# Bank products of a linear-attention memory: 64-row head pairs against 32-row single heads in four row quarters of TensorE

## The reference

```python
sigma_q = elu_plus_one(q)                                   # (b, 16 heads, s, 32)
a_unnorm = jnp.einsum('bhsd,nhde->nbhse', sigma_q, memories)    # 4 banks n, 32x32 per head
norm = jnp.einsum('bhsd,nhd->nbhs', sigma_q, memory_norms)
a = a_unnorm / jnp.clip(norm, EPS, None)[..., None]
a = a * active[:, None, None, None, None]
weights = jax.nn.softmax(bank_weights, axis=-1)
combined = jnp.einsum('nbhse,hn->bhse', a, weights)
out = combined.transpose(0, 2, 1, 3).reshape(b, s, HID) @ Wo.T
```

## Time and profile before

| | |
|---|---|
| median of 3 runs | 1446.71 us (1446.37 to 1449.19) |
| the profiled execution | 1446.95 us |
| its span, first to last instruction | 1445.1 us |
| PE / DVE / POOL / ACT busy | 1400.0 / 876.9 / 544.2 / 509.6 us |
| bank products (L1163) | 768 matmuls of 64x128 by 64x256 |
| DVE's scalings (L910) | 128 of 128x512, 79.5 us |
| PE's granted clock, mean | 0.993 of 2.4 GHz |

### The profile page before, as it was taken

One profiled execution on the slowest core, in us unless ns is written; L12 is line 12 of the kernel. 1 busy time (PEld: TensorE's weight loads), 2 busy tenths in 40 slices (PEclk: granted clock), 3 DMA queues, 4 the chain that ended last, 5 costly groups with the idle time before them and its releaser, 6 DMA issues.

```text
span 1445.1 us, 18902 instructions
## 1 busy us (share of the span) xinstructions
PE 1400.0 (97%) x6890; PEld 1151.9 (80%) x6890; DVE 876.9 (61%) x1255; ACT 509.6 (35%) x794; POOL 544.2 (38%) x363
## 2 busy tenths in 40 slices
PE   7999999998989999999999999999999999999997
PEld 6678888887768888888888887878888888888885
DVE  5577777877576546454555557484654555563644
ACT  4546666666631222122221233332212212222221
POOL 0656566666043333131322335462313133232311
PEclk9999999999999999999999999999999999999999
DMA  7302222203420202020110312230202111020102
GB/s 253 106 21 97 87 87 87 87 29 146 151 90 29 95 0 94 0 94 29 65 65 29 113 40 95 88 124 1 95 6 89 59 36 65 29 94 0 65 0 94
DMA packets 24040, 102.41 MB, mean 71 GB/s; under 512 B 3012, under 2 KB 3524, under 8 KB 14284
## 3 DMA queue, kind: packets, MB, share of 16 engines
q1 hardware_dynamic: 24012, 102.05, 19.0%
HBM read 68.47 MB, written 33.57 MB: 71 GB/s over the span
## 4 chain that ended last, share of the span: by engine, by line
PE 79%; DVE 12%; issue 4%; ACT 3%; DMA 1%; POOL 1%; SPq 0%; DVEq 0%; POOLq 0%; ACTq 0%
PE bank L1085 25%; PE bank L1087 25%; PE bank L1086 25%; DVE banks_r L910 2%; PE bank L1113 1%; DVE h_abs L1037 1%; PE bank L1163 1%; DVE combT_lo L879 1%; DVE one_each L1025 1%; PE bank L1104 1%; DVE x_ring L873 1%; PE bank L1173 1%; DVE pair_lo L1019 1%; DVE ln_raw L757 1%; DVE inv_norm L897 1%
## 5 line engine op out<-in xcount | busy, mean ns | idle before, releaser
L1000 DVE TENSOR_TENSOR h_act<-bank,silu_g 128x512 f32<-128x512 f32 x128 | 88.0, 690 | 408.5 <-PE bank L1087 387.8
L444 POOL TENSOR_TENSOR hs_lo<-h_abs,hs_hi 128x512 fp32r<-128x512 f32 x128 | 174.9, 1396 | 417.6 <-ACT hs_hi L661 417.6
L400 POOL TENSOR_TENSOR h_lo<-h_raw,h_hi 128x512 fp32r<-128x512 f32 x64 | 125.1, 1982 | 236.8 <-ACT h_hi L644 236.8
L1085 PE MATMUL bank<-h_hi,up_w_hi 128*128 128x512 f32 x512 | 201.3, 393 | 7.2 <-DVE h_act L1000 6.0
L1085 PE MATMUL bank<-h_hi,gate_w_hi 128*128 128x512 f32 x512 | 200.4, 391 | 5.8 <-ACT silu_g L667 3.0
L1085 PE MATMUL bank<-down_w_hi,hs_hi 128*128 128x512 f32 x512 | 199.8, 390 | 2.9 <-POOL hs_lo L444 2.9
L1086 PE MATMUL bank<-h_lo,up_w_hi 128*128 128x512 f32 x512 | 200.8, 392 | 0.0
L1087 PE MATMUL bank<-h_hi,up_w_lo 128*128 128x512 f32 x512 | 200.5, 392 | 0.0
L1087 PE MATMUL bank<-h_hi,gate_w_lo 128*128 128x512 f32 x512 | 199.6, 390 | 0.0
L1086 PE MATMUL bank<-down_w_lo,hs_hi 128*128 128x512 f32 x512 | 199.5, 390 | 0.0
L1087 PE MATMUL bank<-down_w_hi,hs_lo 128*128 128x512 f32 x512 | 199.5, 390 | 0.0
(11 more groups left out here) (130 smaller groups left out, 2408.0 us busy)
## 6 DMA issues: line engine op xcount, KB each, us to landing
h_raw<-h2T_scratch SPq DMA_DIRECT2D x16, 1024.0 KB, 4.8
x_ring<-in_x_dram SPq DMA_DIRECT2D x8, 1024.0 KB, 4.9
x_scratch<-x_ring SPq DMA_DIRECT2D x8, 1024.0 KB, 3.9
h2T_scratch<-h_full SPq DMA_DIRECT2D x8, 1024.0 KB, 3.9
over_x<-x_scratch SPq DMA_DIRECT2D x8, 1024.0 KB, 4.8
acc_scratch<-over_x SPq DMA_DIRECT2D x8, 1024.0 KB, 3.9
over_x<-acc_scratch SPq DMA_DIRECT2D x8, 1024.0 KB, 4.8
out_dram<-over_x SPq DMA_DIRECT2D x8, 1024.0 KB, 3.9
```

The source lines that it names most:

```text
L400: nc.gpsimd.tensor_tensor(h2_lo[:, k], h2_raw[:, k], h2_hi[:, k].bitcast(F32), ALU.subtract).then_inc(h2_lo_done, 1)
L444: nc.gpsimd.tensor_tensor(hs_lo[:, j], h_abs[:, j], hs_hi[:, j].bitcast(F32), ALU.subtract).then_inc(hs_lo_done, 1)
L1000: nc.vector.tensor_tensor(h_act[:, cc, j], bank[2 * (j % 2) + 1][:], silu_g[:, j % 2], ALU.mult).then_inc(h_done, 1)
L1085: nc.tensor.matmul(out_, stat[0], mov[0], start=start, stop=False)
```

## The change

Each product now contracts the 32 rows of one head. The four heads of a group lie in the four row quarters of the array, and each writes a PSUM bank of its own; the moving operand has 128 columns, four memory banks by 32, without zeros. The loop goes over the four groups g, and each adds a block of 128 columns to all four banks. The layouts of the norms, the gates and of `banks_r` follow. The wait for DVE is now one, for all four scalings, at the start of a run; in the first subtile of a tile there are four waits for the low half of `sigma`, one per group.

```diff
-            mem_hi = sba("mem_hi", [P, K, NB * HALF], F32R)
-            mem_lo = sba("mem_lo", [P, K, NB * HALF], F32R)
+            mem_halves = sba("mem_halves", [P, 4, K, NB * DH], F32R)
+            mem_hi, mem_lo = mem_halves[:, 0], mem_halves[:, 1]
...
                     r = banks_r[s % 2][:].rearrange("p k n c -> p (k n c)").rearrange(
-                        "p (b n c) -> p b n c", n=NB, c=HALF)
+                        "p (b n e) -> p b n e", n=NB, e=DH)
                     for i in range(2):
-                        blocks = slice(i * K, (i + 1) * K)
+                        blocks = slice(i * 2 * K, (i + 1) * 2 * K)
...
-                    nc.gpsimd.tensor_tensor(combined[:].rearrange("p k (b c) -> p (k b) c", c=HALF), r[:, :, 0], r[:, :, 1],
+                    nc.gpsimd.tensor_tensor(combined[:].rearrange("p k (h e) -> p h k e", e=DH),
+                                            r[:, :, 0].rearrange("p (h k) e -> p h k e", k=K),
+                                            r[:, :, 1].rearrange("p (h k) e -> p h k e", k=K),
                                             ALU.add).then_inc(comb_done, 1)
...
-            for pair in range(PAIR * K):
-                ins = nc.vector.tensor_tensor(gate_cols[:, pair],
-                                              bank_sb[:, PAIR * pair:PAIR * (pair + 1)].rearrange("p h n -> p n h"),
-                                              active_sum[:].unsqueeze(2).broadcast_to([P, NB, PAIR]), ALU.mult)
-            link(ins)
+            link(nc.vector.tensor_tensor(bank_gate[:], bank_sb[:],
+                                         active_sum[:].unsqueeze(1).broadcast_to([P, K * HG, NB]), ALU.mult))
...
-                for g in range(K):
-                    dve.wait_ge(banks_done, 4 * u + g + 1)
+                    "p (h g n e) -> p h g n e", h=HG, g=K, n=NB)
+                r = inv.rearrange("p (g h n) -> p h g n", g=K, h=HG)
+                for h in range(HG):
+                    dve.wait_ge(banks_done, 4 * u + h + 1)
                     nc.vector.tensor_tensor(
-                        scaled[:, g // 2, :, g % 2],
-                        bank[g][:].rearrange("p (i a e) -> p i a e", i=2, e=DH),
-                        r[:, g // 2, :, g % 2].unsqueeze(3).broadcast_to([P, 2, NB * PAIR, DH]),
+                        scaled[:, h], bank[h][:].rearrange("p (g n e) -> p g n e", g=K, n=NB),
+                        r[:, h].unsqueeze(3).broadcast_to([P, K, NB, DH]),
                         ALU.mult).then_inc(banks_r_done, 1)
...
             def banks_of(t, s):
                 u = 4 * t + s
                 toks = slice(s * P, (s + 1) * P)
-                for two in range(2):
+                if s > 0:
+                    pe.wait_ge(banks_r_done, 4 * u)
+                for g in range(K):
                     if s == 0:
-                        pe.wait_ge(sigma_lo_done, 4 * t + 2 * two + 2)
-                    else:
-                        pe.wait_ge(banks_r_done, 4 * u - 2 + 2 * two)
-                    for i in range(2):
-                        g = 2 * two + i
-                        cols = slice(i * T // 2, (i + 1) * T // 2)
-                        for stat, mov, first, last in ((sigma_hi, mem_hi, True, False), (sigma_lo, mem_hi, False, False),
-                                                       (sigma_hi, mem_lo, False, True)):
-                            for pair in range(PAIR):
-                                rows = slice(HALF * pair, HALF * (pair + 1))
-                                ins = nc.tensor.matmul(bank[2 * two + pair][:, cols], stat[rows, g, toks],
-                                                       mov[rows, g], start=first, stop=last)
-                                if i == 1 and last:
-                                    ins.then_inc(banks_done, 1)
+                        pe.wait_ge(sigma_lo_done, 4 * t + g + 1)
+                    cols = slice(g * NB * DH, (g + 1) * NB * DH)
+                    for stat, mov, first, last in ((sigma_hi, mem_hi, True, False), (sigma_lo, mem_hi, False, False),
+                                                   (sigma_hi, mem_lo, False, True)):
+                        for h in range(HG):
+                            rows = slice(DH * h, DH * (h + 1))
+                            ins = nc.tensor.matmul(bank[h][:, cols], stat[rows, g, toks], mov[rows, g],
+                                                   start=first, stop=last)
+                            if g == K - 1 and last:
+                                ins.then_inc(banks_done, 1)
```

More of the change, by code:

```diff
@@ L114, in adaln_kernel @@
             norm_raw = sba("norm_raw", [P, K, NB])
-            norm_bd = sba("norm_bd", [P, K, NB, HG])
+            norm_bd = sba("norm_bd", [P, K, HG, NB])
             bank_sb = sba("bank_sb", [P, K * HG, NB])
@@ L118, in adaln_kernel @@
             active_sum = sba("active_sum", [P, NB])
-            bank_gate = sba("bank_gate", [P, K, NB, HG])
+            bank_gate = sba("bank_gate", [P, K * HG, NB])
             inv_norm = sba("inv_norm", [P, 2, K * NB * HG])
@@ L573, in _ @@
             act.wait_ge(mem_bd_ready, 1)
-            nc.scalar.activation(mem_hi[:], xn2[:, :, 0:NB * HALF], ACT.Copy).then_inc(wa_hi, 1)
+            nc.scalar.activation(mem_hi[:], xn2[:, :, 0:NB * DH], ACT.Copy).then_inc(wa_hi, 1)
             sigma_all(0, first=True)
@@ L804, in _ @@
                                     ALU.subtract).then_inc(bank_shifted, 1)
[L807 to L814, removed]
+            mem_bd = xn2[:, :, 0:NB * DH].rearrange("p k (n e) -> p k n e", n=NB)
             for hh in range(HG):
                 rows = slice(DH * hh, DH * hh + DH)
-                nc.vector.tensor_copy(norm_cols[rows, :, hh // PAIR, :, hh % PAIR], norm_raw[rows])
+                nc.vector.tensor_copy(norm_bd[rows, :, hh], norm_raw[rows])
             dve.wait_ge(bank_exp, 1)
@@ L844, in _ @@
                     rows = slice(DH * hh, DH * hh + DH)
-                    pair, h = hh // PAIR, hh % PAIR
-                    ins = nc.vector.tensor_tensor(mem_bd[rows, k, :, h, :], mem_raw[rows, k],
-                                                  gated(rows, PAIR * k + pair, h), ALU.mult)
+                    ins = nc.vector.tensor_tensor(mem_bd[rows, k], mem_raw[rows, k],
+                                                  bank_gate[rows, HG * k + hh].unsqueeze(2).broadcast_to([DH, NB, DH]),
+                                                  ALU.mult)
                 h1_low(0, k)
@@ L850, in _ @@
             dve.wait_ge(wa_hi, 2)
-            nc.vector.tensor_tensor(mem_lo[:], xn2[:, :, 0:NB * HALF], mem_hi[:].bitcast(F32), ALU.subtract).then_inc(gate_ready, 1)
+            nc.vector.tensor_tensor(mem_lo[:], xn2[:, :, 0:NB * DH], mem_hi[:].bitcast(F32), ALU.subtract).then_inc(gate_ready, 1)
             for g in range(K):
@@ L1144, in norms @@
                     ins = nc.tensor.matmul(bank[6][:, cols], sigma[:, g, s * P:(s + 1) * P],
-                                           norm_bd[:, g].rearrange("p n h -> p (n h)"), start=True, stop=True)
+                                           norm_bd[:, g].rearrange("p h n -> p (h n)"), start=True, stop=True)
                 ins.then_inc(norm_done, 1)
```

4 lines of the change are left out of this document (removed).

## The result

The change makes the kernel slower: 1459.04 us median (1457.84 to 1460.36, 4 runs) against 1446.54 (1445.42 to 1449.19, 4 runs) of the kernel before on the same chip, a ratio of 1.0079 with a 95% interval of 1.006 to 1.0098. The profiled execution took 1459.17 us, its span 1457.4, at a mean granted clock of 0.973 (before: 1446.95, 1445.1, 0.993). The forecast was 1462.0.

What follows compares the result with a forecast made beforehand. PE was taken to bound the kernel, except from 217 to 227 us of each tile, where DVE sets the end; wait 4.7 plus clock 10.4 made 15.1 us over 1446.95, so 1462 (range 1450.5 to 1467).

Steps and rivals of the forecast that it cites:

- PE's own work: Bank products on PE: steps of four at 0.11, a run 1.32 us against 1.40, 0.08 less.
- C: Rival on bank products: four quarters' loads run two at a time, steps of 0.22, 1474 us; chance 0.07.
- D: Rival, not slower: steps bound by columns, not loads; 1448 at 0.06, 1445.5 at 0.044 or less; chance 0.05.
- The wait: PE and DVE handshake, attention tiles: coarser waits cost 0.66 us a tile, 4.7 us together.
- S1: DVE's scaling of subtile 1 in each tile: starts at 221.54 instead of 220.88, 0.66 us later.
- B1: Bank products of subtile 1 on PE: start at 219.80, not 219.66.
- B0: Bank products of subtile 0 on PE: gain 0.08, which DVE's row swallows.
- The clock: PE's granted clock: a fall per tile likelier than not, 1.4 us in tiles 1 to 6, 10.4 together.
- The sum: Whole kernel: wait 4.7 plus clock 10.4 make 15.1 us, so 1462; chance 0.57.
- Tile 0: First attention tile: wait 0.1 us, clock fall 2.0, as nothing is spare there.
- Tile 7: Last attention tile: the wait costs 0.66 us, as in tiles 1 to 6; no clock price.
- From 226.90 on PE sets it again: Tile 4 before: DVE sets the end from 217 to 227 us, PE from the output product at 226.90.

Runs made afterwards that it cites:

- a_wide: Changed kernel, products of groups 0 to 2 moving 256 columns instead of 128, result the same: 1452.61 us, ratio 1.0035 to the kernel before.
- w_coarse: Kernel before with only the change's coarse handshake, on both PE's and DVE's side: 1453.04 us, ratio 1.0033.
- w_pe: Kernel before with only PE's side of the handshake coarse; DVE may still start after two banks: 1449.01 us, ratio 1.0017.
- w_halfcols: Kernel before, own handshake, each paired product moving 128 of 256 columns (half the bank products left out): 1456.91 us, ratio 1.0059.
- b_reorder: Kernel before, DVE's statistics of the previous tile moved behind the low half of the transposed sum: 1448.43 us, ratio 1.0006.
- b_re2: Kernel before, DVE's statistics behind the transposed sum's low half and ACT's square root behind two affine steps: 1440.40 us, ratio 0.9956.
- b_act: Kernel before, only ACT's square root moved behind the first two affine steps of the next tile's first norm: 1445.10 us, ratio 0.9987.

## Why the prediction came out right

The direction, the two causes and the place were right; the sum, 15.1 us against 12.3 in the span, was as close in part by luck. Of the 12.3, 1.55 lie in the second phase, where the forecast had 0 and where no run shows a cost of the change. In the attention phase 10.7 us stand against 15.1, and there a fall longer than forecast and a wait that vanished behind it cancelled in part.

- **PE's own work**: steps of four were forecast at 0.11, measured 0.112; rivals C and D are out. A run is 1.28 us for the forecast 1.32: its first step is 0.16, not 0.22. The kernel before ran 1.42. The Trainium skill ("TensorEngine Tiling (Array Packing)", Theoretical Speedup) gives up to 2 times for a small dimension of 64 or less and up to 4 times for 32 or less, so up to 2 from the one to the other, as an estimate from its two figures. The runs show 1.28 for 1.42 us, and 1.29 with half the columns in two halves: from two to four quarters nothing was won beyond what the narrower products gave.
- **The wait**: S1 was forecast 0.66 late in a tile, it was 0.51. B1 started where forecast (5.52 behind B0); the run was 0.04 shorter, and DVE started 0.31 behind the last step's start, not 0.42. Alone it costs 0.6 to 0.7 a tile (a_wide, w_coarse), as the sum said. Its split was wrong: of the 0.66, 0.14 were PE's late start, and w_pe shows that this by itself is free.
- **The clock**: held for likelier than not, and it came in each tile. Three things in the step were off. A fall lasts 6.8 us, not 3.4. Its price was forecast at 1.4 a tile and is 4.9 in six tiles, 0.8 each (1.26 in tile 1, 0.6 to 0.7 in the last three). And it was put down to pauses and half-streamed products together: w_halfcols shows that the latter suffice, w_coarse that pauses alone don't.
- **The sum**: adding the two terms was the step that failed. In the low clock PE's transposes, not DVE's low half, end last before the output product, so the wait of 0.5 vanishes behind them. 0.66 + 1.4 = 2.1 a tile was forecast; 1.9 to 1.2 were measured, 8.4 us in six tiles for 12.4.
- **Tile 0** was forecast at 2.1 and took 3.02 longer, with a fall of 10.2 us. Up to 0.9 of that may be a matter of the execution, as the 44.7 us of b_reorder and b_re2 show.
- **Tile 7** stood in the sum with 0.66 and is 0.26 shorter up to the second phase: S1 and the output product are 0.51 late there too, but the product had a pause of 2.17 before it, of which 0.66 are left.
- **The second phase** was forecast as unchanged. PE is busy in it for 1053.63 of 1075 us, against 1052.64 in a stretch as long before, and it lasts 1.55 longer; the scatter of the fourteen traces is wider.
- **The setup** was taken at 0, at most 0.5 to be won: it is 0.44 shorter. No gain is shown by that: among the ten executions of the last section with the shorter setup it lasts 48.80 to 49.23 us with the changed kernel's setup and 48.67 to 49.09 with the old one.
- **"From 226.90 on PE sets it again"** was incomplete. A second chain from the same DVE row, over ACT's square root, ended just as late. It left the forecast alone, since all that the change delayed stood ahead of both; it would have ruined a forecast for b_reorder, and did.

## What to carry to other kernels

Where the load of the stationary operand bounds the step, splitting a product into narrower ones that run side by side wins little: 0.13 us a run here, off the path. It also halves the columns that each product streams, and here that cost the clock; with the columns restored, even useless ones, the clock held in four tiles of six, and the two short falls cost nothing. A bank that completes only at the end of a run turns the overlap of two engines into turns: count what stands behind the later engine's row. And where several chains leave the same row, shortening one shows nothing until the others are shortened too: look for an engine that stands at a wait in front of work that others need.

## What had not been expected of the hardware

In the setup the same products ran at either clock in different executions. Timeline of PE in the profiled execution of w_coarse; in that of the kernel before the first two of these products are at 26.56 and 27.12 and last 0.77 and 0.63:

```profile
26.77 0.47 PE L1085 MATMUL bank<-h_hi,wq_hi 128*128 128x512 f32 x1 [0.22 <-DVE h_lo L780]
27.08 0.40 PE L1086 MATMUL bank<-h_lo,wq_hi 128*128 128x512 f32 x1
27.32 0.39 PE L1087 MATMUL bank<-h_hi,wq_lo 128*128 128x512 f32 x1
```

The next starts 0.24 later here, 0.43 there. In the kernel before, the spacing goes over from 0.43 to 0.24 at 36.4 us:

```profile
35.85 0.63 PE L1085 MATMUL bank<-h_hi,wq_hi 128*128 128x512 f32 x1
36.28 0.43 PE L1086 MATMUL bank<-h_lo,wq_hi 128*128 128x512 f32 x1
36.55 0.40 PE L1087 MATMUL bank<-h_hi,wq_lo 128*128 128x512 f32 x1
36.79 0.40 PE L1085 MATMUL bank<-h_hi,wq_hi 128*128 128x512 f32 x1
```

The trace's record of the granted clock begins at just that time, at 2.4 GHz. For a stretch ahead of it the views print 1.00, though the spacing there is that of 1.2 GHz; so the clock of a setup is to be read from the products. The record begins at 35.2 to 36.4 us in four of the fourteen profiled executions (before, after, w_halfcols, b_act), and B0 of tile 0 starts at 50.6 to 51.0 there. In the other ten it begins at 26.2 to 32.1 us, and B0 starts at 48.7 to 49.2, whatever the kernel. The 1.9 us between the setups go with this later rise. Timed runs of the kernel before spread from 1444.4 to 1451.3 us, wide enough to hold it. What decides when the clock rises isn't shown.

The clock fell in the changed kernel where PE had been busy for 3.23 of the last 3.40 us, and didn't in tile 4 of w_coarse with pauses of 0.90 and 0.77. The Trainium skill ("TensorE: Matmul & The Clock Gate", Why this matters for your kernels) asks for no long idle gaps of PE between bursts of matmuls, to keep the throughput from dropping. Here that was not enough: no wait of PE in tiles 1 to 6 of these runs reached 1.1 us, and the clock fell all the same. w_halfcols shows it with nothing changed but the columns that the products stream.
